# A nine-point local attention in one fused kernel: the value products split by key rows into two half arrays

## The chip, the cores and the metric

The kernel runs on one NeuronCore of a Trainium2 chip. The metric is the time of the whole program on the device in microseconds (us), from a batch of 16 images in device memory to the batch of outputs there. Five engines work side by side: PE (TensorE, matmuls; its weight loads are listed apart as PEld), DVE (VectorE), ACT (ScalarE), POOL (GpSimd) and SP (SyncE, which issues the DMAs here). Each has its own list of instructions and they wait for one another through semaphores.

## What is computed

For each of 16 images of 32 x 32 pixels and 128 channels:

```
perceived = depthwise 3x3 conv of x, three filters a channel, + b_perc
hid  = gelu(w_up1 . perceived + b_up1)                  # 384 -> 256 channels
h    = x + w_up2 . hid + b_up2                          # 256 -> 128 channels
q, k, v = w_qkv . h + b_qkv
scores[pixel, i] = q[pixel] . k[neighbour i] / sqrt(C)  # 9 neighbours, zero-padded borders
w    = softmax(scores over the 9 neighbours)
out  = h + sum_i w[pixel, i] * v[neighbour i]
```

## The kernel before

One image is one stage of a software pipeline. In the body of image n, three images are in flight: the convolution of image n, the attention of image n-1 (scores and softmax) and the value products and the output of image n-2. The bodies 0 to 3 are written out, 4 to 13 are a loop of two bodies, and 14, 15 and 16 are written out again. The order of the work on each engine is the order of the code in that engine's `body`; nothing reorders it, and a wait stops everything that stands behind it on that engine.

**Convolution.** Depthwise filter and `w_up1` are folded into one set of weights, kept as a high and a low fp32r part (`whi`, `wlo`). PE's `unit(n, par, i)` adds nine products of 128 x 256 (line 373) into a half bank of `m_ps`; twelve units make an image, numbers 0 to 5 for the first 128 hidden channels and 6 to 11 for the second. DVE puts the units together (`combine`, lines 722 and 723; `combine_y`, lines 732 to 738; `finish_y`, line 746) and ACT applies the gelu (line 533).

**Attention.** `up` (line 388) makes `h` in `work` banks 0 and 1, and DVE's `sum_h` (line 815) takes it. `project_v` (line 399), `project_q` (line 394) and `scores` (lines 408 and 412) fill `work` and `s_ps`. Line 412 works on a quarter of the array's columns at a time (32 of 128). After the exponential (ACT, line 590) POOL normalises (line 908), DVE transposes 32 x 32 blocks (line 787) and ACT puts them at their places in `pt` (line 581). Tile i of `pt` holds on its 128 partitions the pixels of four image rows as keys (partition = key), and in its free dimension the weights that queries of six image rows (192 columns) give to those keys. They are zero but for neighbours.

**Value products.** `values(n, hp, g)` (line 430) makes the output channels of 16 image rows (g = 0 the upper half, g = 1 the lower). The result has 512 columns, one PSUM bank: `work` bank 2 for g = 0 and bank 0 for g = 1. Each of the five key tiles that touch these 16 rows gives one fp32 product: 128 keys deep and 160, 192, 192, 160 and 32 columns wide (for g = 1 the same, from the narrow one on). `values` of g = 0 stands between units 9 and 10, that of g = 1 between units 10 and 11.

**Around it.** On DVE, one body ends with `turn_p(n, 1)` (line 787), `finish_y(n, 1)` (line 746) and two `add_h` (line 796), which add `h` to each bank and write `o_sb`; each raises `o_done`. The next body begins with `transform_ab` (lines 648 and 650), then `combine` (line 722). On PE, after unit 11 come units 0 to 3 of the next image and then `up`. `up` writes `work` banks 0 and 1, so it waits for `hid_done` (the gelu of the second half) and, from image 3 on, for `o_done` to count both `add_h` of the body before.

Of the kernel before, what the change touches and what calls it, by code (L numbers as in the profile page):

```python
# [14 lines left out]
P = 128  # L15
B, H, W, C = 16, 32, 32, 128
PIX = H * W
TR = P // W
T = H // TR
CH = 512  # L20
# [63 lines left out]
def build(nc, x_planes, x_rows, w_perc, b_perc, w1_c, b_up1, w2_c, b_up2, wqk_c, wv_c, b_qkv, ident_bf_c,  # L84
          mask_c, zero_c, out):
    with ExitStack() as ctx:
# [3 lines left out]
        def sem(name):  # L90
            return ctx.enter_context(nc.semaphore(name))
# [129 lines left out]
        ptc_done = sem("ptc_done")  # L221
        pt_done = sem("pt_done")
        pn_last_done = sem("pn_last_done")
        o_done = sem("o_done")

        fcge_done = sem("fcge_done")
# [36 lines left out]
                return (m_ps[:, 0, :], m_ps[:, 1, :], work[:, 2, :], work[:, 0, :])[part]  # L263
            return work[:, (1, 2, 0, 1)[part], :]

        def o_bank(n, g):

            if isinstance(n, int) and n >= B:
                return (m_ps[:, 2, :], work[:, 1, :])[g]
            return work[:, (2, 0)[g], :]  # L270

        def s_bank(g):

# [59 lines left out]
        def _(pe):  # L333
# [82 lines left out]
            def values(n, hp, g):  # L416

                pe.wait_ge(v_done, n * 4 - 4)
                pe.wait_ge(pt_done, n * PLACED - PLACED)
                if not isinstance(n, int) or n < B:  # L420

                    pe.wait_ge(z_done, n * 4 - 2 + g)
                elif n > B:
                    pe.wait_ge(o_done, n * 2 - 5 + g)
                half = T // 2 * TR
                blocks = [(i, max(i * TR - 1, g * half), min((i + 1) * TR + 1, (g + 1) * half)) for i in range(T)]
                blocks = [(i, first, end) for i, first, end in blocks if first < end]
                for i, first, end in blocks:
                    above = i * TR - 1
                    last = pe.matmul(o_bank(n, g)[:, (first - g * half) * W:(end - g * half) * W], v_sb[:, hp, i, :],  # L430
                                     pt[:, i, (first - above) * W:(end - above) * W], start=(i == blocks[0][0]),
                                     stop=(i == blocks[-1][0]), skip_group_check=True)
                last.then_inc(o_ready, 1)

            def last_attention(n, par):
# [195 lines left out]
        def _(dve):  # L631
# [157 lines left out]
            def add_h(n, hp, g):  # L789

                cols = slice(g * CH, (g + 1) * CH)
                dve.wait_ge(o_ready, n * 2 + (g - 3))
                if from_image(n, 3):

                    dve.wait_ge(stored[g], n * 16 - 32)
                nc.vector.tensor_tensor(o_sb[:, cols], o_bank(n, g), h[:, hp, cols], ALU.add).then_inc(o_done, 1)

            def normalise_last(n):

# [171 lines left out]
```

## Time and profile before

| | |
|---|---|
| time, median of 3 runs | 445.86 us (444.5 to 446.4) |
| time of the profiled execution | 446.29 us |
| its span, first to last instruction | 444.5 us |
| busy: PE, DVE, ACT, POOL | 409.7, 346.5, 274.4, 175.7 us |
| one image in the steady part (image 7 to 8) | 24.79 us |

The span is 1.8 us shorter than the profiled execution's own time; what lies around the span is the same for any version of this kernel. A matmul's record begins when its stream may begin and is longer than the stream (it holds the way through the array), so records of PE overlap, and the distance between the starts of two records is the time that one takes from the next. An fp32 matmul in the code appears as two records, each with a weight load of its own. Lines of the profile are lines of the kernel before.

### The profile page before, as it was taken

To read this page: it belongs to the slowest core of one execution; us is meant where nothing else is said; L and a number is where in the kernel's file an instruction comes from. 1 tells how busy PE (TensorE), PEld (TensorE's weight loads), DVE (VectorE), ACT (ScalarE), POOL (GpSimd) and SP (SyncE) were. 2 spreads that over 40 slices of the span, in tenths; PEclk is the share of its full clock that TensorE was granted. 3 is DMA by queue.
4 is the path that set the end of the run, shared out by engine and by line. 5 is a ranking of instruction groups with operands and counts; after the bars stand their busy time and mean duration, and the time that the engine had idled before them with its cause. 6 is when DMAs were issued, how large, how long until landed. Compare 5 with 4: busy or idle time off the path is not lost.

```text
span 444.5 us, 9702 instructions
## 1 busy us (share of the span) xinstructions
PE 409.7 (92%) x3572; PEld 348.9 (78%) x3572; DVE 346.5 (78%) x641; ACT 274.4 (62%) x645; POOL 175.7 (40%) x152
## 2 busy tenths in 40 slices
PE   1397998999999999999999999999999999999754
PEld 1397695988889797988889797979888797979444
DVE  4997669797988979797978989797979889655441
ACT  5414268668475658668475657677575757566661
POOL 5567065252535444352535345352435344101000
PEclk9999899999999999999999999999999999999996
DMA  8210201031311304040311204040312202010111
GB/s 276 95 56 9 111 2 47 1 122 38 110 50 48 113 0 157 0 132 25 110 47 54 103 0 157 0 155 2 110 47 82 75 14 82 2 49 1 48 49 47
DMA packets 11366, 29.20 MB, mean 66 GB/s; under 512 B 2384, under 2 KB 3024, under 8 KB 11344
## 3 DMA queue, kind: packets, MB, share of 16 engines
q1 hardware_dynamic: 10640, 28.89, 18.9%
q8 instruction: 14, 0.23, 0.2%
q10 hardware_dynamic: 704, 0.02, 0.1%
q14 instruction: 8, 0.07, 0.0%
HBM read 20.51 MB, written 8.39 MB: 65 GB/s over the span
## 4 chain that ended last, share of the span: by engine, by line
PE 83%; DVE 7%; issue 6%; ACT 2%; DMA 1%; POOL 1%; POOLq 0%; ACTq 0%; DVEq 0%
PE m_ps L373 43%; PE work L388 12%; PE work L430 9%; PE work L399 6%; PE work L394 6%; PE s_ps L412 5%; PE s_ps L408 1%; ACT pt L581 1%; DVE t L658 1%; DMA wp<-w_perc 1%; PE m_ps L430 1%; DVE y L733 1%; DVE y L736 1%; DVE s_ps L682 1%; ACT hid L533 1%
## 5 line engine op out<-in xcount | busy, mean ns | idle before, releaser
L373 PE MATMUL m_ps<-thi,whi 128*128 128x256 f32 x576 | 181.2, 315 | 5.1 <-POOL wlo L917 4.8
L373 PE MATMUL m_ps<-thi,wlo 128*128 128x256 f32 x576 | 162.9, 283 | 0.0
L373 PE MATMUL m_ps<-tlo,whi 128*128 128x256 f32 x576 | 162.8, 283 | 0.0
L373 PEld LDWEIGHTS m_ps<-thi,whi 128*128 128x128 f32 x576 | 110.0, 191 | 14.7 <-issue 12.0
L373 PEld LDWEIGHTS m_ps<-tlo,whi 128*128 128x128 f32 x576 | 110.0, 191 | 7.2 <-issue 7.2
L373 PEld LDWEIGHTS m_ps<-thi,wlo 128*128 128x128 f32 x576 | 109.8, 191 | 0.0
L533 ACT ACTIVATE hid<-y,b1eff 128x1024 f32<-128x1024 f32 x32 | 36.9, 1152 | 88.9 <-DVE y L746 61.4
L908 POOL TENSOR_TENSOR p_sb<-p_sb,rsum 128x384 f32<-128x384 f32 x31 | 27.0, 871 | 155.5 <-DVE rsum L776 155.5
L901 POOL TENSOR_TENSOR tlo<-t,thi 128x1088 fp32r<-128x1088 f32 (+1 forms) x32 | 64.2, 2030 | 56.9 <-ACT thi L517 56.9
L581 ACT COPY pt<-ptc 32x256 f32<-32x256 f32 (+1 forms) x192 | 76.4, 398 | 7.1 <-DVE ptc L787 2.3
L388 PE MATMUL work<-hid,w2T 128*128 128x512 f32 x120 | 55.8, 609 | 3.6 <-ACT hid L533 3.6
L754 DVE TENSOR_TENSOR v_sb<-work,bv 128x256 f32<-128x256 f32 x62 | 23.7, 415 | 35.3 <-PE work L399 35.3
L430 PE MATMUL work<-pt,v_sb 128*128 128x192 f32 (+2 forms) x300 | 47.1, 305 | 0.0
L590 ACT ACTIVATE p_sb<-s_ps,negmax 128x101 f32<-128x101 f32 x128 | 42.8, 357 | 6.0 <-DVE negmax L769 5.8
L430 PEld LDWEIGHTS work<-pt,v_sb 128*128 128x128 f32 x300 | 45.1, 193 | 0.0
L722 DVE TENSOR_TENSOR ps_sb<-m,m_ps 128x512 f32<-128x512 f32 x32 | 22.0, 688 | 29.5 <-PE m_ps L373 17.2
L388 PEld LDWEIGHTS work<-hid,w2T 128*128 128x128 f32 x120 | 22.3, 195 | 26.6 <-issue 24.9
L517 ACT CAST thi<-t 128x1088 fp32r<-128x1088 f32 (+1 forms) x32 | 26.4, 872 | 26.0 <-DVE t L658 26.0
L733 DVE SCALAR_TENSOR_TENSOR y<-ps_sb 128x256 f32<-128x256 f32 x32 | 41.3, 1291 | 0.0
L732 DVE TENSOR_TENSOR y<-ps_sb 128x256 f32<-128x256 f32 x32 | 38.3, 1196 | 0.0
L399 PE MATMUL work<-wvT,h_around 128*128 128x129 f32 x248 | 35.5, 275 | 0.0
L399 PEld LDWEIGHTS work<-wvT,h_around 128*128 128x128 f32 x248 | 31.7, 191 | 0.9 <-ACT q_sb L609 0.7
(92 smaller groups left out, 592.2 us busy)
## 6 DMA issues: line engine op xcount, KB each, us to landing
xp<-x_planes SPq DMA_DIRECT2D x16, 680.0 KB, 4.5
xr<-x_rows SPq DMA_DIRECT2D x16, 512.0 KB, 3.4
out<-o_sb SPq DMA_DIRECT2D x32, 256.0 KB, 2.1
w1T<-w SPq DMA_DIRECT2D x1, 384.0 KB, 3.3
w2T<-w SPq DMA_DIRECT2D x1, 128.0 KB, 4.9
wqk_in<-w_qk SPq DMA_DIRECT2D x1, 128.0 KB, 4.8
mask_bf<-masks SPq DMA_DIRECT2D x1, 120.0 KB, 3.8
wv_in<-w_v SPq DMA_DIRECT2D x1, 64.0 KB, 4.6
```

Of the source, the lines that this page charges most:

```text
L373: last = pe.matmul(m_ps[:, b, col:col + S], a[:, j, dy, half * P:(half + 1) * P], c[:, par, T_PLACE[j], dy * WIN:dy * WIN + S], start=(s = ...
L388: last = pe.matmul(up_bank(n, c), w2T[:, half * C:(half + 1) * C], hid[:, half, c * CH:(c + 1) * CH], start=(half == 0), stop=(half == 1))
L394: pe.matmul(work[:, b, :], wqk[:, :], h[:, hp, cols], start=True, stop=True).then_inc(q_ready, 1)
L399: last = pe.matmul(v_bank(n, part)[:, u * VT:(u + 1) * VT], h[:, hp, i * P:(i + 1) * P], wvT[:, :], start=True, stop=True)
L430: last = pe.matmul(o_bank(n, g)[:, (first - g * half) * W:(end - g * half) * W], v_sb[:, hp, i, :], pt[:, i, (first - above) * W:(end - ab ...
L533: nc.scalar.activation(hid[:, half, :].rearrange("p (r k s) -> p k r s", k=K4, s=WIN), y[:, half, :, :].rearrange("p k (r s) -> p k r s", ...
L581: nc.scalar.copy(pt[near * W:(near + 1) * W, first + shift:end + shift, col:col + W], ptc[row * W:(row + 1) * W, first:end, dk * W:(dk + 1 ...
L590: nc.scalar.activation(p_sb[:, i, 0:KEYS], s_bank(i // 4)[:, i % 4, 0:KEYS], ACT.Exp, bias=negmax[:, i:i + 1], accum_out=p_sum[:, i:i + 1] ...
L732: nc.vector.tensor_tensor(y[:, half, 0, :], p, s, ALU.add).then_inc(y_part_done, 1)
L733: nc.vector.scalar_tensor_tensor(out=y[:, half, 2, :], in0=s, scalar=4.0, in1=p, op0=ALU.mult, op1=ALU.add).then_inc(y_part_done, 1)
L901: nc.gpsimd.tensor_tensor(tlo[:, par, part, :], t[:, part, :], thi[:, par, part, :].bitcast(F32), ALU.subtract).then_inc(tlo_done, 1)
L908: nc.gpsimd.tensor_tensor(p_sb[:, tiles, 0:NEAR], p_sb[:, tiles, 0:NEAR], rsum[:, tiles].unsqueeze(2).to_broadcast([P, 4, NEAR]), ALU.mult ...
```

## The change

With images below 16 (`is_split`), each key tile's product is made in two parts: part 0 with the upper two key rows (partitions 0 to 63), part 1 with the lower two (partitions 64 to 127). A part is 64 deep and touches four query rows, so it is 128 columns wide in the middle and 96 or 32 at the ends. The parts stand in the two row halves of the array and add into different banks: for g = 0 `work` banks 2 and 0, for g = 1 `work` bank 1 and `s_ps` bank 0. One of each pair (`full`) covers all 512 columns, the other (`inner`) 480. `add_h` becomes two additions: `o_sb = full + h`, then `o_sb += inner` on 480 columns, and the second waits on the new semaphore `o_part_done` for the first. `values` waits for one step more of `z_done`, and for g = 1 also for the first four exponentials of the image in `s_ps` bank 0. The last body (images 14 and 15's values, n = 16 and 17) stays as it was.

```diff
+        def is_split(n):
+            return not isinstance(n, int) or n < B
-        def o_bank(n, g):
+        def o_banks(n, g):
             if isinstance(n, int) and n >= B:
-                return (m_ps[:, 2, :], work[:, 1, :])[g]
-            return work[:, (2, 0)[g], :]
+                return ((m_ps[:, 2, :],), (work[:, 1, :],))[g]
+            return ((work[:, 2, :], work[:, 0, :]), (work[:, 1, :], s_ps[:, 0, :]))[g]
...
-                    pe.wait_ge(z_done, n * 4 - 2 + g)
+                    pe.wait_ge(z_done, n * 4 - 1 + g)
+                    if g == 1:
+                        pe.wait_ge(p_done, n * 8 - 4)
...
-                blocks = [(i, max(i * TR - 1, g * half), min((i + 1) * TR + 1, (g + 1) * half)) for i in range(T)]
-                blocks = [(i, first, end) for i, first, end in blocks if first < end]
-                for i, first, end in blocks:
-                    above = i * TR - 1
-                    last = pe.matmul(o_bank(n, g)[:, (first - g * half) * W:(end - g * half) * W], v_sb[:, hp, i, :],
-                                     pt[:, i, (first - above) * W:(end - above) * W], start=(i == blocks[0][0]),
-                                     stop=(i == blocks[-1][0]), skip_group_check=True)
+                parts = len(o_banks(n, g))
+                by_part = {}
+                rows, keys = TR // parts, P // parts
+                for a in range(parts):
+                    blocks = [(i, max(i * TR + a * rows - 1, g * half), min(i * TR + (a + 1) * rows + 1, (g + 1) * half))
+                              for i in range(T)]
+                    by_part[a] = [(i, first, end) for i, first, end in blocks if first < end]
+                for i in range(T):
+                    for a in range(parts):
+                        for j, first, end in by_part[a]:
+                            if i == j:
+                                above = i * TR - 1
+                                last = pe.matmul(o_banks(n, g)[a][:, (first - g * half) * W:(end - g * half) * W],
+                                                 v_sb[a * keys:(a + 1) * keys, hp, i, :],
+                                                 pt[a * keys:(a + 1) * keys, i, (first - above) * W:(end - above) * W],
+                                                 start=(i == by_part[a][0][0]), stop=(i == by_part[a][-1][0]),
+                                                 skip_group_check=True)
...
-                nc.vector.tensor_tensor(o_sb[:, cols], o_bank(n, g), h[:, hp, cols], ALU.add).then_inc(o_done, 1)
+                if not is_split(n):
+                    nc.vector.tensor_tensor(o_sb[:, cols], o_banks(n, g)[0], h[:, hp, cols],
+                                            ALU.add).then_inc(o_done, 1)
+                    return
+                full, inner = o_banks(n, g)[::1 if g == 0 else -1]
+                some = slice(W, CH) if g == 0 else slice(0, CH - W)
+                o = o_sb[:, cols]
+                nc.vector.tensor_tensor(o, full, h[:, hp, cols], ALU.add).then_inc(o_part_done, 1)
+                dve.wait_ge(o_part_done, n * 2 + (g - 3))
+                nc.vector.tensor_tensor(o[:, some], o[:, some], inner[:, some], ALU.add).then_inc(o_done, 1)
```

PE, the value products of g = 1 in the loop, before (`work` is bank 0):

```order
L422 REGISTER_ALU [waits pt_done,v_done]
L430 MATMUL work<-pt,v_sb 128x32 [waits z_done]
L430 MATMUL work<-pt,v_sb 128x160
L430 MATMUL work<-pt,v_sb 128x192 x2
L430 MATMUL work<-pt,v_sb 128x160
```

and the same place after the change (`s_ps` is its bank 0 and takes part 1, `work` is bank 1 and takes part 0):

```order
L431 REGISTER_ALU [waits z_done,pt_done,v_done]
L447 MATMUL s_ps<-pt,v_sb 128x32 [waits p_done]
L447 MATMUL work<-pt,v_sb 128x96
L447 MATMUL s_ps<-pt,v_sb 128x128
L447 MATMUL work<-pt,v_sb 128x128
L447 MATMUL s_ps<-pt,v_sb 128x128
L447 MATMUL work<-pt,v_sb 128x128
L447 MATMUL s_ps<-pt,v_sb 128x128
L447 MATMUL work<-pt,v_sb 128x128
L447 MATMUL s_ps<-pt,v_sb 128x96
```

Five products became nine, four of part 0 and five of part 1, in turns; nothing else on PE has moved.

DVE, the end of the first body of the loop and the begin of the second, before:

```order
L795 ISA [waits o_ready]
L796 TENSOR_TENSOR o_sb<-work,h_around 128x512 [waits stored0]
L792 REGISTER_ALU
L796 TENSOR_TENSOR o_sb<-work,h_around 128x512 [waits stored1,o_ready]
L644 ISA
L647 REGISTER_ALU [waits x_loaded0]
L648 SCALAR_TENSOR_TENSOR ab<-xp 128x272 [waits tlo_done]
```

and after (lines 822 and 824 are the two additions of `add_h`, line 667 is the old 648):

```order
L814 ISA [waits o_ready]
L822 TENSOR_TENSOR o_sb<-work,h_around 128x512 [waits stored0]
L824 TENSOR_TENSOR o_sb<-o_sb,work 128x480 [waits o_part_done]
L811 REGISTER_ALU
L822 TENSOR_TENSOR o_sb<-s_ps,h_around 128x512 [waits stored1,o_ready]
L824 TENSOR_TENSOR o_sb<-o_sb,work 128x480 [waits o_part_done]
L663 ISA
L666 REGISTER_ALU [waits x_loaded0]
L667 SCALAR_TENSOR_TENSOR ab<-xp 128x272 [waits tlo_done]
```

Two additions became four in a row, each second one behind a wait for the first, and everything behind them on DVE stands two additions later.

## Rows read from the trace of the kernel before

**Rows 1.** The page's chain that ended last: its share of the span by engine.

```profile
PE 83%; DVE 7%; issue 6%; ACT 2%; DMA 1%; POOL 1%; POOLq 0%; ACTq 0%; DVEq 0%
```

**Rows 2.** Busy time by engine, granted clock (third last column), from `up` of image 7 to 8.

```profile
193.44:218.23 24.79, 24.79 (x224) 21.19 (x223) 20.99 (x38) 16.58 (x40) 10.60 (x10) 1.00 0.21 71
```

**Rows 3.** Timeline of PE: start, length, engine, line, form, count; `values` between units.

```profile
208.86 0.28 PE L373 MATMUL m_ps<-thi,wlo 128*128 128x256 f32 x1
208.98 1.50 PE L430 MATMUL work<-pt,v_sb 128*128 128x160 f32 x10
210.31 0.36 PE L373 MATMUL m_ps<-thi,whi 128*128 128x256 f32 x1
...
211.47 1.58 PE L430 MATMUL work<-pt,v_sb 128*128 128x32 f32 x10
212.77 0.39 PE L373 MATMUL m_ps<-thi,whi 128*128 128x256 f32 x1
```

**Rows 4.** Timeline of PE and PEld: column-tiled scores (`128*32`), back to the full array.

```profile
204.46 0.87 PE L412 MATMUL s_ps<-h_around,q_sb 128*32 128x96 f32 x32
205.25 0.19 PEld L373 LDWEIGHTS m_ps<-thi,whi 128*128 128x128 f32 x1
205.36 0.19 PEld L373 LDWEIGHTS m_ps<-tlo,whi 128*128 128x128 f32 x1
```

**Rows 5.** Timeline, from the full array into the column-tiled scores.

```profile
203.13 0.33 PE L408 MATMUL s_ps<-mask_bf,ident_bf 128*128 128x384 bf16 x1
203.39 0.65 PEld L412 LDWEIGHTS s_ps<-h_around,q_sb 128*32 128x32 f32 x32 [0.27 <-issue]
```

**Rows 6.** Groups by line and form, whole span: busy us, mean ns of one record.

```profile
L412 PE MATMUL s_ps<-h_around,q_sb 128*32 128x96 f32 x1024 | 27.8, 249 | 0.0
```

**Rows 7.** Timeline of DVE from unit 9's hand-over to the next image's `combine`.

```profile
209.27 0.69 DVE L722 TENSOR_TENSOR ps_sb<-m,m_ps 128x512 f32<-128x512 f32 x1 [0.92 <-PE m_ps L373]
...
215.19 0.64 DVE L746 TENSOR_TENSOR y<-y,m_ps 128x512 f32<-128x512 f32 x1
215.77 1.27 DVE L796 TENSOR_TENSOR o_sb<-work,h_around 128x512 f32<-128x512 f32 x2
...
218.52 0.69 DVE L722 TENSOR_TENSOR ps_sb<-m,m_ps 128x512 f32<-128x512 f32 x1 [0.79 <-PE m_ps L373]
```

**Rows 8.** Timeline of ACT, PEld and PE: the gelu and `up` of image 8.

```profile
215.87 1.16 ACT L533 ACTIVATE hid<-y,b1eff 128x1024 f32<-128x1024 f32 x1 [4.56 <-DVE y L746]
...
218.12 0.31 PEld L388 LDWEIGHTS work<-hid,w2T 128*128 128x128 f32 x2
...
218.23 3.60 PE L388 MATMUL work<-hid,w2T 128*128 128x512 f32 x8
```

**Rows 9.** Timeline, a DVE instruction that waits for the one before it on DVE.

```profile
204.33 0.25 DVE L765 TENSOR_TENSOR s_ps<-work,z_base 128x10 f32<-128x10 f32 x2 [0.15 <-PE s_ps L412]
204.61 0.58 DVE L769 TENSOR_REDUCE negmax<-s_ps 128x4 f32<-128x404 f32 x1
```

**Rows 10.** Timeline, image 2, where `up` did wait for the gelu.

```profile
68.11 1.15 ACT L533 ACTIVATE hid<-y,b1eff 128x1024 f32<-128x1024 f32 x1 [4.68 <-issue]
...
69.31 0.30 PEld L388 LDWEIGHTS work<-hid,w2T 128*128 128x128 f32 x2 [1.75 <-ACT hid L533]
```

**Rows 11.** Timeline, the second `add_h` and `up` of image 13; both of image 15.

```profile
340.43 0.67 DVE L796 TENSOR_TENSOR o_sb<-work,h_around 128x512 f32<-128x512 f32 x1
342.28 0.59 PE L388 MATMUL work<-hid,w2T 128*128 128x512 f32 x1
388.43 1.28 DVE L796 TENSOR_TENSOR o_sb<-work,h_around 128x512 f32<-128x512 f32 x2
391.90 0.59 PE L388 MATMUL work<-hid,w2T 128*128 128x512 f32 x1
```

**Rows 12.** Timeline, `sum_h` and the `project_v` behind it on PE.

```profile
221.13 1.49 DVE L815 SCALAR_TENSOR_TENSOR h_around<-work,b,xr 128x512 f32<-128x512 f32 x2
223.80 0.61 PE L399 MATMUL work<-wvT,h_around 128*128 128x129 f32 x4
```

More of the change, by code:

```diff
@@ L223, in build @@
         pn_last_done = sem("pn_last_done")
+        o_part_done = sem("o_part_done")
         o_done = sem("o_done")
```

## The prediction

> **What bounds the kernel now.** First the chain that ended last, for the engine that carries the span: PE has 83% of it [rows 1]. Then one steady period, from `up` of image 7 to `up` of image 8: 24.79 us, PE busy throughout at the full clock, DVE busy 20.99 [rows 2]. So a microsecond taken off PE is worth a microsecond, as long as no other engine's loop is longer than PE's. That is the question here, since the change takes from PE (or means to) and gives to DVE. So I then read DVE's timeline around the place of the change [rows 7] and the instruction of PE that waits for it, `up` [rows 8].
>
> There are two branches from the end of unit 9 to the next `up`. PE's: both `values`, units 10 and 11, units 0 to 3. DVE's: `combine` starts at 209.27, after 0.92 us of idleness that PE ended, and from there DVE works without a pause to the end of the second addition at 215.77 + 1.27 = 217.04 [rows 7]. `up` begins its weight load at 218.12 [rows 8]. DVE's branch is thus 218.12 - 217.04 = 1.08 us shorter than PE's. The gelu, the other thing `up` waits for, ends at 217.03 [rows 8]; the change does not touch it.
>
> **PE: what the value products take now.** For g = 0 they run from 208.98 to the convolution's next product at 210.31, whose record is 0.08 longer than the usual 0.28: it waited that long for its weights. That makes 1.33 + 0.08 = 1.41 us. For g = 1: 212.77 - 211.47 = 1.30, and 0.39 - 0.28 = 0.11 more, again 1.41 [rows 3].
>
> **PE: what they take after.** Three prices.
> - Streaming. `up` gives the rate: eight records of 512 columns in 3.60 us, the last one 0.59 long, so (3.60 - 0.59) / 7 = 0.43 us each [rows 8], 0.84 ns a column. A part of 128 columns streams for 0.107 us.
> - Weights. 128 columns of weights took 205.36 - 205.25 = 0.11 us where nothing else held them up [rows 4]. Every record has its own weight load, so a half array can't start records closer than 0.11 us, be they 128 or 32 columns wide.
> - Switching the array between whole and tiled. No row of before shows row tiles; the nearest are the column tiles of the scores. Out of them: the last record starts at 204.46 + 0.87 - 0.25 = 205.08 [rows 4, 6], streams 96 columns (0.08) to 205.16, the next weight load starts only at 205.25, and it is exposed for 0.11: 0.20 us with nothing streaming. Into them: the mask product starts at 203.13 and streams 384 columns in one pass at the full clock (0.16) to 203.29, the load starts at 203.39 [rows 5]; 0.10, and 0.11 for a load of 128 columns, 0.20 again.
>
> If the two halves work side by side, g = 0 has ten records in its busier half: nine steps of 0.11, then 32 columns (0.03), makes 1.02, with both switches 1.42 us, counted from the end of the last convolution stream. Now, on the same count, from 208.86 + 0.11 = 208.97 to 210.31 + 0.08 = 210.39, it is 1.42. **Nothing is gained.** For g = 1 the last record has 96 columns: 0.99 + 0.08 + 0.40 = 1.47 against 212.88 - 211.46 = 1.42. PE's branch grows by about 0.05 us an image.
>
> That the halves do work side by side is taken from the column tiles: 32 records of 96 columns take 0.87 us [rows 4]; one after another they would take 32 x 0.08 = 2.6. Bounds: one after another, the 18 loads of a half image take 8 x 0.11 = 0.88 us more each, 1.8 us an image. Below: if a 64-deep load took half as long, the stream would decide, 512 columns twice (0.86) instead of 1.02 for g = 0, and about 0.2 to 0.4 us an image would be gained on this branch. I take the middle, +0.05, since column tiles are the nearest thing in the trace.
>
> Here stands a rule against that sum: the Trainium skill, "TensorEngine Tiling (Array Packing)", Theoretical Speedup and Key Properties, promises up to 2x for a contraction of 64, and says that changing the mode drains the engine. By the first alone the products would fall from 736 to 512 columns' time; the drain, which [rows 4, 5] show with 0.1 us a side, takes it back.
>
> **DVE: what the additions cost.** One addition moves into two. Now two independent ones take 1.27 us, the second starting about 0.60 after the first (1.27 - 0.67), and 0.67 is one alone [rows 7, 11]. After, a second addition must wait for the end of the first: an instruction that depends on the one before it started 204.61 - (204.33 + 0.25) = 0.03 us after its end [rows 9]. It has 480 columns, with one operand from PSUM and one from SBUF, as `finish_y`, which takes 0.64 for 512 [rows 7]; I take 0.64 as its length and 0.57 as the distance to an independent successor. The chain: 0.67 + 0.03 + 0.57, then 0.67 + 0.03 + 0.64 = 2.61 us instead of 1.27: **1.34 us later**. The added DVE time does not fit in the 1.08 us. Additions end at 215.77 + 2.61 = 218.38; a load of `up` started 0.05 after its releaser ended (68.11 + 1.15 = 69.26 to 69.31) [rows 10]; 218.43 instead of 218.12: `up` waits **0.31 us** in each image.
>
> This wait is a loop: PE's later `up` makes unit 9 later, and DVE starts from there again. So the period becomes 24.79 + 0.31. PE's own growth of 0.05 lies in the parallel branch and is hidden; for the same reason a gain on PE there would bring nothing. The Trainium skill, "TensorEngine Tiling (Array Packing)", PSUM Bottleneck, warns of just this: tiling speeds the array, not the emptying of PSUM. [rows 7, 8] agree, with 1.08 us to spare against 1.34 needed.
>
> How often: `up` waits for `o_done` from image 3 on. Image 13 looks like image 8: the second addition ends at 340.43 + 0.67 = 341.10, `up` starts at 342.28 [rows 11], the same 1.18 that image 8 has from 217.04 to 218.23. At image 15 the additions end at 389.71 and `up` starts at 391.90 [rows 11], 2.19 us later: DVE's branch is a microsecond shorter there, and 1.34 fits. In image 16 `up` uses `m_ps` and doesn't wait for the additions. That leaves images 3 to 14: 12 x 0.31 = 3.7 us, and 0.05 to 0.1 for the images where PE's branch decides.
>
> **What else moves.** Behind the additions on DVE stand `ab`, then `combine`, which idled 0.79 us before 218.52 [rows 7]; it takes up 0.79 of 1.34 and starts about 0.5 later. `transform` and `sum_h` shift with it: `sum_h` ended at 222.62 and PE's `project_v` begins its load at about 223.68, 1.06 later [rows 12]. With PE itself 0.31 later, the shift of 0.5, and even some tenths more, costs nothing there. The new waits of `values` are free: on DVE the last z term, and the reciprocal that itself waits for the first four exponentials, stand before `combine`, and DVE was idle for 0.92 us before 209.27 [rows 7]; so both are done by 208.35, before the products at 208.98 and 211.47 [rows 3].
>
> **Rivals.**
> - *DVE's additions just fit.* If the dependent addition costs no more than an independent one (0.57 to 0.60 each), the delay is 1.14 to 1.2 and `up` waits 0.1 to 0.17: 12 x 0.13 = 1.6 us, 447.5. For it: the length of the second addition is known from a neighbour only. Against: the 0.03 and the lost overlap are in [rows 9] and [rows 7].
> - *Row tiles do not run side by side.* Nothing in this trace shows a weight load of one row half beside another. 1.8 us an image for 14 images: 25 us, 471. It decides as soon as PE's branch grows by more than 0.31.
> - *They do, but each switch costs more* than with column tiles (0.2 to 0.4 more a `values`): PE's branch grows 0.4 to 0.9, 14 times: 452 to 458.
> - *Faster.* If the additions stayed off the path (their 1.34 under 1.08) and row halves needed neither drain nor the 0.11 a load: 736 to 512 columns at 4 x 0.42 ns is 0.38 us for each half image, 28 of them: -10.5 us, 435. It takes both at once, and the first contradicts [rows 7, 8].
>
> **How the numbers follow.** Forecast (`up` waits 0.2 to 0.5 us): 0.62. Additions just fit: 0.12. Switches cost more: 0.12. No concurrency: 0.11. Faster: 0.03. The profiled execution takes 446.3, and the forecast for it is 450.1; from the median, 445.9 + 3.8 = **449.7 us**. The forecast's own ends: 12 x 0.2 and 12 x 0.5, 448.3 to 452. The range, with the just-fit case and the dearer switches, is **447 to 458**; it leaves out no concurrency and faster. Half a percent (2.2 us), about what a measurement can tell, divides the forecast from the just-fit case: faster 0.03, same 0.13, slower 0.84.
>
> **What would show it.** PE: a wait of about 0.3 us before line 388's weight load, released by DVE's second addition, in 12 images and none in image 15. Ten starts 0.11 apart in one row half, with the other half's starts within 0.01 of them; 0.1 us without a load at each switch. DVE: four additions in 2.6 us, its idle time before `combine` of 0.79 gone. I am wrong if `up` does not wait, if the first convolution product behind `values` comes more than 0.3 us later than now, or if the row halves' records alternate at a distance of 0.11.

## The result, and the profile after

The changed kernel takes **452.4 us** (median of 4 runs, 450.6 to 453.1) against 446.1 (444.5 to 448.0, 4 runs) for the kernel before, a ratio of 1.0125 with an interval of 1.0083 to 1.0166 (here and below the ratio is taken over all runs and is not that of the two medians). A repeat on another occasion gave 452.4 against 444.7, 1.0143 (1.0106 to 1.0181). It is slower, as forecast, and in the range, but by 6.2 and 7.7 us between the medians rather than 3.8. The profiled execution takes 452.0 (span 450.2), 5.7 more than that of before.

The page's busy times, the chain that ended last (shares of the span), and the granted clock in 40 slices, to be held against [rows 1]:

```profile
PE 415.3 (92%) x3796; PEld 345.6 (77%) x3796; DVE 333.9 (74%) x669; ACT 272.4 (60%) x645; POOL 185.5 (41%) x152
...
PE 81%; issue 6%; DVE 3%; ACT 1%; POOL 0%; POOLq 0%; ACTq 0%
...
PEclk9999999999999999999999999999999999999886
```

The steady period from `up` of image 7 to `up` of image 8, columns as in [rows 2]:

```profile
194.50:219.63 25.13, 25.11 (x239) 20.90 (x239) 19.21 (x41) 16.34 (x40) 11.61 (x9) 1.00 0.21 69
```

25.13 instead of 24.79, at the full clock. From `up` of image 2 to `up` of image 14 it is 370.69 - 68.72 = 301.97 us, before 367.07 - 69.31 = 297.76: **4.21 us in 12 images, 0.35 each**. PE still looks busy throughout (25.11 of 25.13), and a list of PE's waits shows none for the additions: the ends of the records are modelled and bridge the gap. The stall is seen only in the weight load of `up` (in brackets: idle before it, and what ended it) and in the distance from the last convolution start, 0.30 instead of 0.12:

```profile
219.33 0.28 PE L380 MATMUL m_ps<-thi,wlo 128*128 128x256 f32 x1
219.63 2.84 PE L395 MATMUL work<-hid,w2T 128*128 128x512 f32 x6
...
219.62 0.30 PEld L395 LDWEIGHTS work<-hid,w2T 128*128 128x128 f32 x2 [0.23 <-DVE o_sb L824]
```

(`x6` of the eight records of `up`, since the window ends there.) DVE's timeline at the same place, the counterpart of [rows 7]:

```profile
216.36 0.64 DVE L765 TENSOR_TENSOR y<-y,m_ps 128x512 f32<-128x512 f32 x1
216.93 0.67 DVE L822 TENSOR_TENSOR o_sb<-work,h_around 128x512 f32<-128x512 f32 x1
217.63 0.65 DVE L824 TENSOR_TENSOR o_sb<-o_sb,work 128x480 f32<-128x480 f32 x1
218.20 0.68 DVE L822 TENSOR_TENSOR o_sb<-s_ps,h_around 128x512 f32<-128x512 f32 x1
218.92 0.65 DVE L824 TENSOR_TENSOR o_sb<-o_sb,work 128x480 f32<-128x480 f32 x1
219.57 0.44 DVE L667 SCALAR_TENSOR_TENSOR ab<-xp 128x272 f32<-128x272 f32 x1
...
220.28 0.68 DVE L741 TENSOR_TENSOR ps_sb<-m,m_ps 128x512 f32<-128x512 f32 x1
...
221.47 1.10 DVE L677 SCALAR_TENSOR_TENSOR t<-fc 128x272 f32<-128x272 f32 x2
```

The four additions take 216.93 to 219.57, **2.64 us** (1.27 before); the load of `up` starts 0.05 after. The idle time before `combine` (L741) is gone. The first two `t` operations take 1.10, where they took 0.79: POOL was at work on `t` beside them until 221.92.

PE around `values` for g = 0 and in the middle of g = 1, the counterpart of [rows 3]; `64*128` is a row half. In the last four rows `s_ps` is the lower half and `work` the upper:

```profile
210.02 0.28 PE L380 MATMUL m_ps<-thi,wlo 128*128 128x256 f32 x1
210.23 1.30 PE L447 MATMUL work<-pt,v_sb 64*128 64x96 f32 x18
211.46 0.39 PE L380 MATMUL m_ps<-thi,whi 128*128 128x256 f32 x1
...
213.15 0.27 PE L447 MATMUL s_ps<-pt,v_sb 64*128 64x128 f32 x1
213.15 0.27 PE L447 MATMUL work<-pt,v_sb 64*128 64x128 f32 x1
213.26 0.27 PE L447 MATMUL s_ps<-pt,v_sb 64*128 64x128 f32 x1
213.26 0.27 PE L447 MATMUL work<-pt,v_sb 64*128 64x128 f32 x1
```

The halves' records start in pairs, 0.11 after the pair before. Counted as in the prediction, from the end of the last convolution stream (210.02 + 0.11) to the next product's stream (211.46 + 0.11), g = 0 takes 1.44; g = 1, worked out the same way (213.99 - 212.50), 1.49. The busier half has ten records, one every 0.11 us, and with the two switches that comes to what the ten wider records of the whole array took, 1.42: nothing is won.

**The rest of the difference is the clock.** The last stretch, `up` of image 16 to the end: the kernel after, then the kernel before; and then the first piece of it in both, where `up` (eight records) is alone on PE:

```profile
418.45:450.20 31.75, 19.89 (x134) 14.02 (x134) 10.34 (x23) 14.80 (x43) 0.83 (x1) 0.77 0.13 50
414.67:444.50 29.83, 17.93 (x134) 13.16 (x134) 9.18 (x21) 14.80 (x43) 0.83 (x1) 0.87 0.14 53
...
418.45:423.90 5.45, 5.37 (x8) 1.99 (x8) 1.96 (x4) 4.66 (x12) 0.00 (x0) 0.69 0.26 96
414.67:418.40 3.73, 3.67 (x8) 1.40 (x8) 0.78 (x2) 3.51 (x10) 0.00 (x0) 1.00 0.38 141
```

The same eight products took 5.37 us at a mean granted clock of 0.69 (part of them at 1.2 GHz) and 3.67 at 1.00 (2.4 GHz). In both kernels PE had waited 2.10 us for the gelu just before. These 1.7 us, 1.9 with the rest of the stretch, come from the clock and not from added work. Whether the change makes the low clock likelier is another question, taken up at the end of the experiments. The span's 5.7 us are then: 0.6 less until `up` of image 2 (68.72 for 69.31), 4.2 in the loop, 0.2 in the two images behind it, and 1.9. Each run also lists its mean granted clock, so all runs of this study can be sorted by it (mean us, number of runs; two more of before, at 0.991, took 444.5):

```
mean granted clock   0.980 or 0.981  0.984          0.987 or 0.988
kernel before        448.24 (13)     446.25 (13)    444.61 (34)
kernel after         452.56 (8)      450.48 (2)     -
```

At an equal clock the change costs 4.2 to 4.3 us; the step from one clock group to the next costs 1.6 to 2.1. The kernel after was in the lowest group in 8 of its 10 runs, the kernel before in 13 of 62.

### The profile page after: what moved, and what is told of

Its sections match the earlier page's. It is cut to its first block, busy times and chain, and to the rows that moved or that the text cites. A ratio compares the mean times of both kernels' runs of the same rounds, so it can differ in the third digit from the quotient of the medians.

```text
span 450.2 us, 10182 instructions
## 1 busy us (share of the span) xinstructions
PE 415.3 (92%) x3796; PEld 345.6 (77%) x3796; DVE 333.9 (74%) x669; ACT 272.4 (60%) x645; POOL 185.5 (41%) x152
## 4 chain that ended last, share of the span: by engine, by line
PE 81%; issue 6%; DVE 3%; ACT 1%; POOL 0%; POOLq 0%; ACTq 0%
PE m_ps L380 41%; PE work L395 13%; PE work L406 6%; PE work L401 6%; PE s_ps L419 5%; PE work L447 5%; PE s_ps L447 3%; PE s_ps L415 1%; ACT pt L600 1%; PE m_ps L447 1%; DVE y L752 1%; DVE y L755 1%; ACT hid L552 1%; DVE y L757 0%; DVE ps_sb L741 0%
## 5 line engine op out<-in xcount | busy, mean ns | idle before, releaser
L929 POOL TENSOR_TENSOR tlo<-t,thi 128x1088 fp32r<-128x1088 f32 (+1 forms) x32 | 74.5, 2348 | 50.8 <-ACT thi L536 50.8
L773 DVE TENSOR_TENSOR v_sb<-work,bv 128x256 f32<-128x256 f32 x62 | 25.6, 420 | 59.0 <-PE work L406 58.5
L395 PE MATMUL work<-hid,w2T 128*128 128x512 f32 x120 | 57.0, 618 | 4.0 <-ACT hid L552 3.6
L447 PE MATMUL work<-pt,v_sb 64*128 64x128 f32 (+4 forms) x384 | 38.7, 284 | 0.0
L741 DVE TENSOR_TENSOR ps_sb<-m,m_ps 128x512 f32<-128x512 f32 x32 | 21.9, 684 | 18.8 <-PE m_ps L380 10.5
L447 PEld LDWEIGHTS work<-pt,v_sb 64*128 64x128 f32 (+1 forms) x384 | 34.0, 190 | 1.9
L922 POOL TENSOR_TENSOR t<-ab 128x272 f32<-128x272 f32 x16 | 12.4, 772 | 51.4 <-DVE ab L669 51.4
L755 DVE SCALAR_TENSOR_TENSOR y<-ru_sb 128x256 f32<-128x256 f32 x32 | 31.7, 991 | 0.0
```

Of the source, the lines that this page charges most:

```text
L395: last = pe.matmul(up_bank(n, c), w2T[:, half * C:(half + 1) * C], hid[:, half, c * CH:(c + 1) * CH], start=(half == 0), stop=(half == 1))
L447: last = pe.matmul(o_banks(n, g)[a][:, (first - g * half) * W:(end - g * half) * W], v_sb[a * keys:(a + 1) * keys, hp, i, :], pt[a * keys: ...
L755: nc.vector.scalar_tensor_tensor(out=y[:, half, 3, :], in0=u, scalar=8.0, in1=r, op0=ALU.mult, op1=ALU.add).then_inc(y_part_done, 1)
L929: nc.gpsimd.tensor_tensor(tlo[:, par, part, :], t[:, part, :], thi[:, par, part, :].bitcast(F32), ALU.subtract).then_inc(tlo_done, 1)
```

## The experiments

**Experiment 1: is it the second addition?** The kernel after without it; o_sb then lacks the inner bank's half of the products. PE's part of the change stays whole.

```diff
-                nc.vector.tensor_tensor(o, full, h[:, hp, cols], ALU.add).then_inc(o_part_done, 1)
-                dve.wait_ge(o_part_done, n * 2 + (g - 3))
-                nc.vector.tensor_tensor(o[:, some], o[:, some], inner[:, some], ALU.add).then_inc(o_done, 1)
+                nc.vector.tensor_tensor(o, full, h[:, hp, cols], ALU.add).then_inc(o_done, 1)
```

> The changed kernel without the second addition of each output half; the result leaves out the half of the value products that stands in the other bank. My theory (DVE's additions make up wait, PE's products cost about what they did): the additions of a body end 1.3 us earlier, up no longer waits, and only PE's own growth of about 0.1 us an image is left (1.44 + 1.50 us for the two value products in the changed kernel's trace against 2 x 1.42), so 14 x 0.1 = 1.4 us over before, about 447.5, ratio 1.003. Rival (the split products themselves cost the time, through switches of the array): the time stays at about 452, ratio 1.012.

Measured: 447.7 against 445.8, ratio 1.0037 (1.0005 to 1.0069). The steady period, 24.84 us:

```profile
193.50:218.34 24.84, 24.84 (x240) 20.83 (x239) 21.01 (x38) 16.57 (x40) 10.59 (x10) 1.00 0.20 70
```

Averaged over 12 images 24.87, against 24.81 before: PE's own part is **+0.05 an image**, as the prediction's sum said, and `up` waits for nothing. That is half of the 0.1 of the expectation, whose 447.5 was met with the help of the clock: 5 of the 10 runs were in the lowest group. At equal clocks this version takes 0.3 to 0.6 us more than the kernel before.

**Experiment 2: the addition alone.** The kernel before, with unsplit products, and after each addition a second one on 480 columns that depends on it and reads the same bank (o_sb then holds those products twice).

```diff
+                nc.vector.tensor_tensor(o, o_bank(n, g), h[:, hp, cols], ALU.add).then_inc(o_part_done, 1)
+                dve.wait_ge(o_part_done, n * 2 + (g - 3))
+                nc.vector.tensor_tensor(o[:, some], o[:, some], o_bank(n, g)[:, some], ALU.add).then_inc(o_done, 1)
```

> The kernel before, products undivided, with a second addition of 480 columns that waits for the first; it adds the same bank once more, so the output has the value products twice in those columns. My theory: up waits about 0.35 us in images 3 to 14 as in the changed kernel, 12 x 0.35 = 4.2 us, about 450.3, ratio 1.009 to 1.010. Rival (the split products cost the time): within 1 us of before.

Measured: 450.6 (448.5 to 453.0), ratio 1.0144 (1.0118 to 1.0169), period 25.18. The load of `up` of image 8:

```profile
218.11 0.30 PEld L389 LDWEIGHTS work<-hid,w2T 128*128 128x128 f32 x2 [0.29 <-DVE o_sb L805]
```

The addition alone makes the whole slowdown (4.0 to 4.3 us at equal clocks), and PE's +0.05 is hidden under it, as forecast. The two runs together show the cause from both sides.

**Experiment 3: take the wait away.** If `up` had room, the price should be PE's 0.05. `up` runs in two halves of which each overwrites only one pair of banks, so that half c need only wait for the additions of g = c:

```diff
-                        pe.wait_ge(o_done, n * 2 - 4)
+                        pe.wait_ge(o_done, n * 2 + (c - 5))
```

> The changed kernel, but each up waits only for the additions of the bank it writes: up of chunk 0 (bank 0) for those of g = 0, up of chunk 1 (bank 1) for those of g = 1. My theory: the additions of g = 0 end at about 1.3 us after they start, where the two additions of before ended, so the first up doesn't wait, and the second comes 1.7 us later and doesn't wait either; the period falls from 25.16 to about 24.9 us, and what is left is PE's growth of 0.1 us an image: about 447.5, ratio 1.003. Rival (something else that came with the longer DVE branch holds PE, such as h or q coming late): no faster than 450.

Measured: 451.3, ratio 1.0134 (1.0104 to 1.0164), period still 25.15 from image 4 on. **This missed.** `up` waits no longer, and next to nothing is gained (at the lowest clocks 452.3 against 452.6). ACT and PE in the period behind `up` of image 8:

```profile
219.57 3.60 PE L395 MATMUL work<-hid,w2T 128*128 128x512 f32 x8
...
228.48 0.71 PE L406 MATMUL work<-wvT,h_around 128*128 128x129 f32 x4
...
223.53 1.65 ACT L536 CAST thi<-t 128x1088 fp32r<-128x1088 f32 x2 [2.20 <-DVE t L677]
225.21 2.50 ACT L600 COPY pt<-ptc 32x256 f32<-32x256 f32 x6
227.74 0.69 ACT L628 ACTIVATE q_sb<-work,bq_s 128x512 f32<-128x512 f32 x1
```

`project_v` starts at 228.48, 0.05 after the first q copy ends (228.43), the same hand-over distance as at `up`; in the kernel before it was 227.04, with 0.8 to spare. And the q copy follows without a gap on the scatter of `pt` (2.50), that on `thi` (1.65), and that waited for DVE's `t`, the last thing behind the additions, `ab` and `combine`. So there are **two loops of about 25.16**: additions to `up`, and additions to `t` to `thi` to `pt` to q to `project_v`. The second has 1.34 us of additions in it as well, and 0.3 more in the first `t` operations. In the kernel after itself only `up` waits: there the first q copy ends at 228.28 and `project_v` starts at 228.51, so that loop has nearly 0.2 to spare. Once `project_v` does wait, it also takes longer, 1.12 us to the scores' first product (228.48 to 229.60) instead of 0.95 (228.51 to 229.46), and that uses up the 0.2.

**Experiments 4 and 5: fewer switches.** On top of that edit: both `values` behind unit 10, one switch in and one out, to gain 0.4 to 0.6 on PE. Beside it, the same reordering of the kernel before, which has no switches to save.

```diff
                 units(8, 9)
-                if store:
-                    values(n, par, 0)
                 units(10)
                 if store:
+                    values(n, par, 0)
                     values(n, par, 1)
```

> As the one before, and the value products of g = 0 and g = 1 stand next to each other behind unit 10, so the array is switched to half arrays once an image instead of twice. One pair of switches less is 0.4 us an image, and the two halves can even out (18 records each where each g alone has 10 and 8), up to 0.2 more. My theory: the period is 24.3 to 24.6 us against 24.8 of before, 3 to 7 us less in all: 439 to 443, ratio 0.985 to 0.993. Rival (switches are cheap and the weight loads set the time): no faster than the one before, ratio 1.00 or more. A second rival: DVE's chain from unit 9 to the gelu of the second half, now only about a microsecond shorter than PE's, becomes the longer one; then up waits for the gelu and the gain stops at about 24.5.

> The kernel before with one edit: its undivided value products of g = 0 and g = 1 stand next to each other behind unit 10. No array switch is saved, since there is none; the four short records come together. My theory of the adjacent split kernel (its gain on PE is the saved pair of switches and the evened halves): here nothing changes, period 24.75 to 24.85 us, within 1 us of before. Rival (adjacency itself helps): 24.5 us or less.

Measured: split 448.8, ratio 1.0078 (1.0053 to 1.0103); unsplit 444.8 against 444.7, 0.9992 (0.9964 to 1.0021), period 24.76. The split kernel gained less than expected. Its first image with the new order has a period of 24.47, where the same image of experiment 3 has 24.96, so sharing the switches does give back 0.5; then the second loop catches PE: the next period is 24.98, and from there they average 25.15, with PE waiting in the open:

```profile
225.84 1.29 PE L406 MATMUL work<-wvT,h_around 128*128 128x129 f32 x8 [0.20 <-ACT q_sb L627]
```

**Experiment 6: does the alternation matter?** The kernel after with the loop over the parts outside: all records of the upper half, then all of the lower.

```diff
-                for i in range(T):
-                    for a in range(parts):
+                for a in range(parts):
+                    for i in range(T):
```

> The changed kernel with all products of part 0 of a half image first and then all of part 1, instead of in turns. Theory (PE issues in order and the halves overlap only where neighbours in the list use different halves): each half image takes 8 more steps of 0.105 us, 0.84, so 1.7 us an image on PE's branch, of which DVE's longer branch hides 0.3: period 26.5 us, about 470 in all, ratio 1.05. Rival (each row half has its own queue, deep enough to look over ten records): no change against the changed kernel, 452.

Measured: 462.0, ratio 1.0367 (1.0317 to 1.0417), period 25.98: between what the two theories gave. PE, values of g = 1, where the parts go to different tensors (`work`: upper, `s_ps`: lower):

```profile
216.00 0.82 PE L447 MATMUL work<-pt,v_sb 64*128 64x96 f32 x5
216.55 0.29 PE L447 MATMUL s_ps<-pt,v_sb 64*128 64x32 f32 x1
216.66 0.27 PE L447 MATMUL work<-pt,v_sb 64*128 64x128 f32 x1
...
216.88 0.27 PE L447 MATMUL work<-pt,v_sb 64*128 64x128 f32 x1
216.99 0.92 PE L447 MATMUL s_ps<-pt,v_sb 64*128 64x128 f32 x7
217.83 0.38 PE L380 MATMUL m_ps<-thi,whi 128*128 128x256 f32 x1
```

The lower half begins at 216.55, when the upper has three records left to start. From there they overlap; before that the lower half is empty. Side by side needs the halves in turns in the instruction list.

**Experiments 7 and 8: move the additions out of the loop.** The second additions go into the next body, behind the first `take_v`; `up` waits only for the first ones, and the inner banks are both in `s_ps`, so the scores wait for the second ones. Once with adjacent `values`, once without.

```diff
+                        if part == 0 and from_image(n, 3) and not is_last(n):
+                            add_inner(n - 1, 0)
+                            add_inner(n - 1, 1)
...
+                if from_image(n, 3) and not is_last(n):
+                    pe.wait_ge(o_done, n * 2 + (g - 5))
                 s = s_bank(g)[:, :, 0:NEAR]
```

> The split, adjacent products, with the second additions moved out of the two loops they lengthen: the banks are given out so that up of chunk 0 waits for no addition and up of chunk 1 for the first addition of g = 1 alone, and both second additions of an image stand in DVE's idle time of the next body, behind the first take_v. My theory (two loops through DVE, each about 25.15 us long with the second additions in them, held the kernels so far; without, both are under 24.6): PE is the bound again with a period of 24.4 to 24.5 us, as the first such image of the adjacent kernel had (24.47), 13 x 0.34 = 4.4 us less than before at the same clock: about 441.5, ratio 0.990. Rival (another loop, of POOL or ACT, stands at 24.8 or more): no faster than before.

> The same with the value products of g = 0 and g = 1 at their old places, between units 9, 10 and 11, so with two pairs of switches an image. My theory: PE is the bound with a period of 24.86 us, as in the kernel without second additions, so 0.5 to 1 us over before at the same clock: ratio 1.001 to 1.003. Rival (second additions cost time wherever they stand on DVE): 450 or more.

Measured: 451.8, ratio 1.0144 (1.0105 to 1.0183), and 459.1, 1.0307 (1.0269 to 1.0344); periods 25.42 and 25.91. **Both missed** by 10 us and more; by its number the second looks like its rival, additions that cost time wherever they stand, but the rows show a narrower cause. The second of them, DVE, POOL and PE:

```profile
227.87 2.78 DVE L752 TENSOR_TENSOR y<-ps_sb 128x256 f32<-128x256 f32 x1
230.57 1.56 DVE L753 SCALAR_TENSOR_TENSOR y<-ps_sb 128x256 f32<-128x256 f32 x1
...
233.66 1.20 DVE L829 TENSOR_TENSOR o_sb<-o_sb,s_ps 128x480 f32<-128x480 f32 x2
...
227.85 4.01 POOL L942 TENSOR_TENSOR tlo<-t,thi 128x1088 fp32r<-128x1088 f32 x2 [3.26 <-ACT thi L537]
...
234.36 0.34 PE L417 MATMUL s_ps<-mask_bf,ident_bf 128*128 128x384 bf16 x1 [0.93 <-DVE o_sb L829]
```

The scores wait 0.93 us in each of 12 images. I had placed the additions in idle time that DVE has there in the kernel after (2.29 us before 229.16). It is there because POOL's `tlo` starts (224.58) behind DVE's first `y` operation (224.52), and the four `y` operations take 0.41 each. In experiment 8 `tlo` starts first (227.85 against 227.87), two of the `y` operations take 2.78 and 1.56, and the idle time is gone. The kernel before has the same long pair (2.74 and 1.56). The order went with `t` being late in the kernel after and on time in the other two; that the one makes the other is read from these traces and was not tested by itself.

**Experiments 9 to 11: leave DVE one addition.** From here the aim was a version that keeps the split. On the split kernel with adjacent `values`: ACT copies the inner bank to SBUF (`in_sb`), POOL adds h to it (`hin_sb`), and DVE makes one addition as before the change.

```diff
+                        nc.scalar.copy(in_sb[:, g * CH:(g + 1) * CH][:, some], inner[:, some]).then_inc(in_done, 1)
...
+                        nc.gpsimd.tensor_tensor(hin_sb[:, cols], in_sb[:, cols], h[:, par, cols],
+                                                ALU.add).then_inc(hin_done, 1)
...
+                nc.vector.tensor_tensor(o_sb[:, cols], full, hin_sb[:, cols], ALU.add).then_inc(o_done, 1)
```

> The split, adjacent products, but DVE has one addition a half again: ACT copies the inner bank to SBUF in its idle time before the gelu of the second half, POOL adds h to that copy in its idle time, and DVE adds this sum to the full bank. My theory (PE's branch is 24.47 us in the adjacent kernel, and only the second additions on DVE hide that): no loop through DVE is longer than before, the period is 24.45 to 24.55 us, about 4.4 us less than before at the same clock, ratio 0.990. Rival (POOL's two additions, about 1 us each beside DVE's work on y, slow DVE as its other work there does, 0.4 us an operation growing to 1.0 to 1.6): DVE's chain from unit 9 to the gelu grows by more than the 0.75 us that it has, up waits for it, and the period is 24.8 or more.

Measured: 445.8 against 444.7, ratio 1.0007 (0.9979 to 1.0034); the period fell to 24.63, but the ratio not as expected. At equal clocks this is 0.4 to 1.5 us less than before (5 of its 12 runs were in the lowest group), where the loop alone would give more. Most of what was gained in the loop went at its end:

```profile
411.15 1.19 PE L398 MATMUL m_ps<-hid,w2T 128*128 128x512 f32 x1 [3.93 <-ACT hid L554]
```

PE waits 3.93 us there, 2.10 in the kernels before and after. The gelu in question is the last one, in body 15, and it waits for DVE's `y`; two of the four `y` operations run beside POOL's new additions and take 1.50 and 1.48 where they took 0.41 each in the kernel after:

```profile
405.81 1.50 DVE L767 SCALAR_TENSOR_TENSOR y<-ru_sb 128x256 f32<-128x256 f32 x1
407.23 1.48 DVE L769 SCALAR_TENSOR_TENSOR y<-ru_sb 128x256 f32<-128x256 f32 x1
...
405.65 2.77 POOL L974 TENSOR_TENSOR hin_sb<-in_sb,h_around 128x512 f32<-128x512 f32 x2
...
409.86 1.15 ACT L554 ACTIVATE hid<-y,b1eff 128x1024 f32<-128x1024 f32 x1 [3.29 <-DVE y L777]
```

So body 15's second additions went back to DVE (experiment 10; its expectation gives the same wait from the weight load's side, 2.26 and 4.09), and then the scatter of two key tiles, 2.50 us of the second loop, behind the q copies (experiment 11):

```diff
-                if store:
+                if store and is_last(n):
                     place_p(n, (2, 3))
...
+                if store and not is_last(n):
+                    place_p(n, (2, 3))
                 if conv:
                     gelu(n, 0)
```

> The kernel with ACT's copy and POOL's addition, but in body 15 the two additions of a half both stand on DVE as in the changed kernel. In that body nothing else of POOL runs beside DVE, up of image 16 uses other banks and waits only for the gelu, and there the new POOL additions slowed DVE's y and so the gelu: PE's wait before up of image 16 grew from 2.26 to 4.09 us. My theory: that wait is back at 2.3, the period stays 24.63, together 1.8 us less than the version before, 3 to 4 us under before at the same clock: ratio 0.992 to 0.995. Rival (the wait has another cause): no change against the version before, ratio 1.000.

> The same, and ACT places the last two key rows of p (2.5 us) behind the two q copies instead of ahead of them. In the adjacent and the ACT-and-POOL kernels PE's project_v started 0.05 us after the first q copy ended, which is a wait: the loop unit 9, DVE, t, ACT's thi, place, q, PE. My theory: that loop loses 2.5 us, PE is the bound with 24.47 us a period, 0.16 less than 24.63, 2 us in all: ratio 0.988 to 0.991. Rival (the exponentials, now up to 0.5 us later, hold the copy of m13 and with it combine, or DVE's additions hold up): 24.6 or more.

Measured: 443.2, ratio 0.9920 (0.9886 to 0.9954), the wait back at its old length (2.10) and the period 24.64; and **440.4** (438.2 to 442.2, 6 runs), ratio **0.9869** (0.9838 to 0.9900), period 24.37. The last one beats both kernels, the kernel before by 6.1 to 6.3 us at equal clocks. Its period, and PE at both `values`:

```profile
189.25:213.61 24.36, 24.36 (x240) 20.51 (x239) 18.52 (x39) 17.58 (x42) 14.33 (x12) 1.00 0.21 72
...
205.74 0.28 PE L388 MATMUL m_ps<-thi,wlo 128*128 128x256 f32 x1
205.95 1.16 PE L455 MATMUL work<-pt,v_sb 64*128 64x96 f32 x16
...
208.15 0.39 PE L388 MATMUL m_ps<-thi,whi 128*128 128x256 f32 x1
```

Both `values` take 208.15 - 205.74 = 2.41 us, where the kernel after has 1.44 + 1.49 = 2.93. That is where the row halves first pay: not by a faster record (each half still makes one in 0.11) but because the records of the two half images run into one another, so that each half makes 18 in a row instead of twice ten steps, and one pair of switches is gone. The same moves of ACT's and POOL's work were not tried on the unsplit kernel; with PE busy for all of its 24.79 us, there was no wait in its loop for them to remove. `project_v` has 1.0 us to spare over the q copy, `up` 1.4 over the additions.

**The clock, once more.** The kernel after again, to tell a longer loop from a lower clock.

> The changed kernel once more, to have it beside many runs of before at the same mean granted clock. Theory (the loops through DVE cost 0.35 us in 12 images, and the mean clock of a run, 0.980 to 0.988, moves every version alike by up to 4 us): 4.0 to 4.6 us over before at each clock. Rival (the change also costs granted clock): the clocks of its runs lie lower than those of before, and the medians differ by more than the runs at equal clock do.

Both are in it: six runs, 450.4 to 453.1, five of them at a mean granted clock of 0.980. At equal clocks the distance to the kernel before is 4.2 to 4.3 us (the table above), which is the loop; the rest of the 6.2 and 7.7 us between the medians comes with the clock. Why the kernel after falls to the lowest group more often was not found. The second addition alone (experiment 2) had two runs at 0.980 and 0.981 and four at 0.984 and above, so the longer loop by itself does not force it.

What a step between the groups is can be read in the kept traces. `up` of image 1 and `up` of image 16 each follow a wait of PE for the gelu (2.0 to 2.1 us; 3.93 in experiment 9), and the eight products then take either 3.67 us, all at 2.4 GHz, or 5.2 to 5.4 with most of it at 1.2 GHz (6.7 once, in experiment 6). At 0.991 (experiments 2 and 11) both took 3.67. In the trace of the kernel before (0.987) and of experiment 8 (0.988) only the first was slow; in both traces of the kernel after and in experiments 1, 3 and 10 (0.980 and 0.981) both were. A step of 1.6 to 2.1 us is thus about what one slow `up` costs, 1.7 us. The mean clock is not a perfect measure of it: in experiments 5 and 7 (0.984) only the first `up` was slow, and the low clock in the last 20 us lasted about 10 us instead of 7; the trace of the kernel after has this longer stretch too, and there it cost only the 0.2 between the 1.7 and the 1.9 above. What decides in a run whether the clock falls at `up`, no run shows.

## Why the prediction was right or wrong

- **What bounds the kernel: right.** DVE's branch passed PE's, and the loop grew by the excess, in 12 images. At image 15 the additions still had 0.81 us to spare, and its period changed by only 0.1 (24.83 to 24.93).
- **PE's values, 1.42 and 1.47: right.** Measured 1.44 and 1.49, which would be +0.09; the period of experiment 1 gives +0.05 an image. The step of 0.11 a record and the 0.20 of a switch, both taken from column tiles [rows 4, 5], held for row halves: from the last convolution start plus its stream (210.13) to the first load (210.23) 0.10, then 0.11 of exposed load. The rival "dearer switches" fell, and so did "no concurrency": it costs 1.1 us an image even in experiment 6, where the order forbids most of the overlap.
- **The dependent additions, 2.61: right.** Measured 2.64. The distances 0.70, 0.57 and 0.72 are those put together from [rows 7, 9]; "just fit" fell.
- **The stall, 0.31: slightly small.** 0.35. The additions' 0.03 accounts for most: the term was 1.34 less 1.03 of room, and the room was right. Times 12: 4.2 instead of 3.7.
- **"The shift of 0.5, and even some tenths more, costs nothing": the step that failed in its reasoning.** It is true of `sum_h`, which I looked at (its margin fell from 1.06 to 0.59: it ends at 224.59, the load of `project_v` starts at 225.18). I did not follow the other thing that shifts, `t`, to its end: ACT's `thi`, the scatter and the q copy stand in a row behind it, with 0.8 us of margin, not 1.06, and POOL's work beside `t` adds 0.3. This loop came out within 0.2 us of the one I priced, and no longer, so the sum did not suffer; that it did not was luck, since no row had been read for it. The prediction's picture (one wait, all else free) did suffer: by it experiment 3 should have given 447.5, and it gave 451.3.
- **"The new waits of `values` are free": right.** PE waits nowhere at L447 in the loop.
- **The total, 449.7 against 452.4: 2.7 too low.** 452.4 lies just above the forecast's own ends (448.3 to 452) and where the rival of dearer switches had its numbers (452 to 458); it is the experiments, not the time, that decide for the forecast. 0.5 of the 2.7 is the stall; the other 2 is the clock, which I took as given. The median of the kernel before lay in a middle group, most runs of the kernel after in the lowest.

The speedup that the Trainium skill promises ("TensorEngine Tiling (Array Packing)", Theoretical Speedup: up to 2x for a contraction of 64) does not show in any run here: with loads of 0.11 us for 128 columns in each half, the half image took as long as before.

## What to carry to other kernels

When work is added to an engine off the critical path, list everything queued behind it there and follow each item to the engine that waits for it; the shortest margin decides, and there may be two of the same size, so that removing the first wait gains nothing. A split that shortens the streams gains nothing where the weight loads already set the pace, and the switches into and out of it should be shared by as much work as possible. Idle time in a trace is free room only if it stays when the edit changes the timing of the other engines. Before runs are compared by their medians, sort them by granted clock.

## What the runs showed of the hardware

- Two row halves of 64 x 128 load and stream in fp32 at full pace side by side, a pair every 0.11 us, the second within 0.01 of the first, but only with their records in turns. In sequence they overlapped only for the last three or so records of the first.
- Who starts first matters between DVE and POOL. The same DVE operation, 128x256 from SBUF, took 0.41 us or 2.66 to 2.78 beside POOL's `tlo`. Where `tlo` began 0.11 to 0.15 us ahead of DVE's first `y` operation, as in 7 of 13 images of the kernel before, that operation was held every time. Where DVE's first operation began 0.04 to 0.06 ahead, it was never held, and the ones behind it ran free in 9 of 10 images of the kernel after's loop, but in only 4 of 10 of experiment 11; in the others the second took 2.7. With all four free, `tlo` took 5.04 instead of 4.01. A start of `tlo` 0.02 to 0.05 ahead went either way. `y` operations with an operand in PSUM stayed at 0.64 to 0.68. The Trainium skill, "SBUF — State Buffer", Who interferes with whom, says that the order of issue decides which of two such operations holds the shared ports and which one waits. The traces agree where the two starts are 0.11 us apart or more; within 0.06 us the starts in the records do not tell who will be held.
- A run's mean granted clock came in steps (0.980, 0.984, 0.987 and 0.988), 0.980 to 0.984 to 0.987 worth 2.0 and 1.6 us of 446 here, close to half of what was to be measured. In the kept traces the eight products of `up`, behind a wait of 2.0 to 2.1 us, took 5.3 to 5.4 us at the lower clock or 3.67 at the full one, in different runs of much the same code. Comparing at equal clocks gave 4.2 and 4.3 us where the medians gave 6.2 and 7.7.
